# A vision transformer tower on one core: embeddings brought forward, statistics moved to ScalarE, and the first MLP projection from 16-bit halves

## The reference

```
h = concat(class_token, patches @ W.T + b) + pos      # 32 x 37 tokens of 256
x = layernorm(h)
xn = layernorm(x) * ln1_w + ln1_b
q, k = elu(xn @ q_w.T + q_b) + 1, elu(xn @ k_w.T + k_b) + 1 ; v = xn @ v_w.T + v_b   # 16 heads of 16
kv = einsum('bhnd,bhne->bnde', k, v)                  # per token, over the heads
attn = einsum('bhnd,bnde->bhne', q, kv) / einsum('bhnd,bnd->bhn', q, k.sum(heads))
x = x + attn @ o_w.T + o_b
x = x + gelu(( layernorm(x) * ln2_w + ln2_b ) @ fc_w.T + fc_b) @ proj_w.T + proj_b   # MLP, 1024 wide
h = h + x
y = layernorm(h)
scores = softmax(y @ gate_w.T)                        # 16 experts, each takes its top 148 tokens
h = h + experts(y, scores) + shared(y)                # shared: gelu(y @ Sg.T) * (y @ Su.T) @ Sd.T
```

## Time and profile before

| | |
|---|---|
| median of 3 runs | 496.38 us (496.05 to 496.83) |
| the profiled execution | 499.83 us, of which span 498.0 us |
| mean granted clock of TensorE | 0.956 |
| busy, TensorE / its weight loads | 460.0 (92%) / 403.5 (81%) |
| busy, VectorE / ScalarE / GpSimd | 361.9 (73%) / 224.2 (45%) / 150.9 (30%) |
| chain that ended last, by engine | PE 63%, DVE 17%, ACT 5%, issue 5%, DMA 3% |

### The profile page before, as it was taken

The page is one execution under the profiler, slowest core; times in us unless marked ns, Lnnn a source line. Parts: engine busy times, 40 slices in busy tenths (PEclk is TensorE's granted clock), DMA queues, the critical chain, the costliest instruction groups (busy, mean ns, idle before and its releaser), DMA issues.

```text
span 498.0 us, 10363 instructions
## 1 busy us (share of the span) xinstructions
PE 460.0 (92%) x3853; PEld 403.5 (81%) x3853; DVE 361.9 (73%) x674; ACT 224.2 (45%) x527; POOL 150.9 (30%) x252
## 2 busy tenths in 40 slices
PE   7989899999999999899897899899999999999990
PEld 3547678888888888779776679799999999999990
DVE  1289998999999999721398698588876677777720
ACT  1431364664754752324241005555555666565520
POOL 1311032142142221221000052254665444433432
PEclk9988799999999999999699799899999999999995
DMA  7956101101000000000000018977879888898321
GB/s 240 381 219 270 35 1 35 41 4 45 11 6 7 12 11 12 1 11 23 7 2 0 0 30 289 350 283 279 284 282 308 325 326 326 310 323 320 102 28 13
DMA packets 17348, 69.12 MB, mean 139 GB/s; under 512 B 4338, under 2 KB 10399, under 8 KB 12834
## 3 DMA queue, kind: packets, MB, share of 16 engines
q1 hardware_dynamic: 12130, 61.96, 33.3%
q0 software_dynamic: 4608, 5.41, 5.3%
q10 hardware_dynamic: 576, 1.29, 0.7%
HBM read 63.32 MB, written 5.33 MB: 138 GB/s over the span
## 4 chain that ended last, share of the span: by engine, by line
PE 63%; DVE 17%; ACT 5%; issue 5%; DMA 3%; POOL 1%; DVEq 0%; ACTq 0%; POOLq 0%
PE bank L1409 18%; PE bank L1420 13%; PE bank L1182 5%; PE bank L1196 5%; PE bank L1126 4%; DVE qkt L796 4%; PE bank L1211 3%; PE bank L1316 3%; DMA wex_s<-in_wex 3%; DVE scratch L962 3%; DVE scratch L791 2%; PE bank L1141 2%; PE bank L1170 1%; DVE late L810 1%; PE bank L1431 1%
## 5 line engine op out<-in xcount | busy, mean ns | idle before, releaser
L1420 PE MATMUL bank<-scratch,wex_s 128*128 128x148 f32 x512 | 78.6, 297 | 0.2 <-DVE scratch L1054 0.2
L504 POOL DMA_INDIRECT out_rows<-scratch,slot_s x32 | 52.9, 1652 | 85.3 <-DMA out_rows<-scratch,slot_s 64.7
L1420 PEld LDWEIGHTS bank<-scratch,wex_s 128*128 128x128 f32 x512 | 68.4, 192 | 0.5 <-DVE scratch L1054 0.5
L493 POOL DMA_INDIRECT xg<-token_rows,slot_g x32 | 42.1, 1314 | 76.9 <-DVE slot_g L1027 68.1
L725 ACT ACTIVATE scratch<-bank 128x296 f32<-128x296 f32 x64 | 26.6, 416 | 67.7 <-PE bank L1409 67.7
L421 POOL TENSOR_SCALAR tmp<-mv 128x1 f32<-128x1 f32 x30 | 6.7, 223 | 166.0 <-DVE mv L781 166.0
L1409 PE MATMUL bank<-scratch,wsh_s 128*128 128x148 f16 x512 | 53.5, 229 | 0.0
L1409 PE MATMUL bank<-scratch,wfc_s 128*128 128x148 f16 x512 | 52.6, 227 | 0.0
L1409 PE MATMUL bank<-scratch,wproj_s 128*128 128x148 f16 x256 | 50.6, 227 | 0.0
L945 DVE SCALAR_TENSOR_TENSOR wproj_s<-wex_s,wfc_s 128x512 f16<-128x512 f32 x64 | 40.4, 683 | 12.5 <-ACT wfc_s L708 12.5
L1054 DVE SCALAR_TENSOR_TENSOR scratch<-bank,scratch 128x296 f32<-128x296 f32 x64 | 29.4, 460 | 26.4 <-ACT scratch L725 26.0
(11 more groups left out here) (162 smaller groups left out, 907.3 us busy)
## 6 DMA issues: line engine op xcount, KB each, us to landing
wex_s<-in_wex SPq DMA_DIRECT2D x16, 2048.0 KB
wex_s<-in_wex SPq DMA_DIRECT2D x16, 1024.0 KB
patch_s<-in_patches SPq DMA_DIRECT2D x10, 384.0 KB
token_rows<-y_s SPq DMA_DIRECT2D x10, 128.0 KB, 1.7
out_rows<-h_all SPq DMA_DIRECT2D x5, 256.0 KB
wfc_s<-in_wfc SPq DMA_DIRECT2D x1, 1024.0 KB, 5.1
wproj_s<-in_wproj SPq DMA_DIRECT2D x1, 1024.0 KB, 7.1
wsh_s<-in_wsh SPq DMA_DIRECT2D x1, 1024.0 KB, 8.7
```

The source lines that it names most:

```text
L493: gp.indirect_dma_start(xg[b][:], None, rows, bass.IndirectOffsetOnAxis(slot_g[b][:], 0))\
L504: gp.indirect_dma_start(out, bass.IndirectOffsetOnAxis(slot_s[b][:], 0), eo[b], None, compute_op=ALU.add).then_inc(scattered, 16)
L1420: last = pe.matmul(ps_down[k][:, 0:C], wex_s[s.par][:, lo:lo + P], hexT[:, m, :], start=(m == 0), stop=(m == MC - 1))
```

## The change

It does four things.

1. Embeddings come early, through two PSUM banks in turn (`ps_tok(t)` is bank 7 for odd tiles, else bank 0): tiles 2 and 3 ahead of turn 0, 4 to 6 in turn 0, 7 and 8 in turn 1, 9 in turn 2. The keep-busy products behind tile 0's projections go. Router products of tile t-4 go into turn t, and `EARLY` becomes 6.
2. Means and variances move from VectorE to ScalarE: the row sum is the accumulator output of the operation that makes the row (a copy on ScalarE, an addition on VectorE); ScalarE scales it to minus the mean and squares the row with that bias, with a second accumulator output. GpSimd's shift takes one operation less.
3. MLP up works on 16-bit halves: x2 and its weights, scaled by powers of two, are each split into a high and a low half, and three of the four products are summed. The weights are loaded into expert 0's buffer, ScalarE makes the high halves and GpSimd the rests.
4. x2 is transposed in the turn after it is made, ahead of the attention output projection.

```diff
-        EARLY = 7
+        EARLY = 6
-        BESIDE = [6 - r % 2 for r in range(ROUNDS - 1)] + [0]
+        BESIDE = [6] * (ROUNDS - 1) + [0]
...
 @block.sync
             next_patch(Step(0, 2))
+            sp.dma_start(wo_s[:], wo).then_inc(w_in["o"], 16)
+            next_patch(Step(0, 3))
+            sp.dma_start(wfc_raw, wfc.rearrange("p k n -> p (k n)")).then_inc(w_in["fc"], 16)
+            sp.dma_start(wproj_s[:], wproj).then_inc(w_in["proj"], 16)
+            for t in range(4, TILES):
+                next_patch(Step(0, t))
             sp.dma_start(gate_s[:], gate).then_inc(w_in["moe"], 16)
...
+            sp.wait_ge(fclo_made, 2)
             load_gu(Step(0, 0), 0)
...
 @block.gpsimd
+            def rest_of_fc(b):
+                lo, hi = b * nfc // 2, (b + 1) * nfc // 2
+                gp.wait_ge(fchi_made, b + 1)
+                gp.tensor_tensor(wfc16[1][:, lo:hi], wfc_raw[:, lo:hi], wfc16[0][:, lo:hi], ALU.subtract).then_inc(fclo_made, 1)
+            def rest_of_x2(s):
+                gp.wait_ge(x2hi_made, s.times(1, 1))
+                gp.tensor_tensor(x2_16[1][:], x2T[:], x2_16[0][:], ALU.subtract).then_inc(x2lo_made, 1)
...
 @block.scalar
+            def squares(k, t, src, done):
...
+                act.activation(less[:, k, t:t + 1], total[:, k, t:t + 1], ACT.Copy, scale=-1 / D).then_inc(mean_made, 1)
+                act.wait_ge(mean_made, means)
...
+                act.activation(beside[:], src, ACT.Square, bias=less[:, k, t:t + 1],
+                               accum_out=spread[:, k, t:t + 1]).then_inc(done, 1)
             def copy_h(s):
                 act.wait_ge(tok_done, s.times(1, 1))
-                act.activation(h_all[:, s.n, :], ps_tok[:, 0:D], ACT.Copy).then_inc(h_copied, 1)
+                act.activation(h_all[:, s.n, :], ps_tok(s.n)[:, 0:D], ACT.Copy, accum_out=total[:, 0, s.n:s.n + 1]).then_inc(h_copied, 1)
+                act.wait_ge(h_copied, s.times(1, 1))
+                squares(0, s.n, h_all[:, s.n, :], a_stats)
+            def halve_fc():
+                act.wait_ge(w_in["fc"], 16)
+                for b in range(2):
+                    lo, hi = b * nfc // 2, (b + 1) * nfc // 2
+                    act.activation(wfc16[0][:, lo:hi], wfc_raw[:, lo:hi], ACT.Copy, scale=SPLIT)
+                    act.activation(wfc_raw[:, lo:hi], wfc_raw[:, lo:hi], ACT.Copy, scale=SPLIT).then_inc(fchi_made, 1)
             def turn_x2(s):
...
+                act.activation(x2_16[0][:], x2T[:], ACT.Copy).then_inc(x2hi_made, 1)
...
+            def turn(t, soon=(), late_on=(), blocks=()):    # ScalarE's order
+                turn_attn(t-1); norm_a(t+2); scale_xh(t+2); copy_v(t+1); turn_x2(t-2); squares_f(t-3)
+                negate_qk(t+1); exp_qk(t+1); halve_fc() if t == 0; gelu(t-2); copy_h(soon)
+                squares_c(t-1); norm_f(t-3); turn_xn(t+2); turn_y(t-3); copy_h(late_on)
+                gelu_shared(blocks); load_exp() if 2 <= t < TILES - 2; norm_c(t-1)
...
 @block.vector
-            a_moments, c_moments, f_moments
+            def add_attn(s):
+                ve.wait_ge(o_done, s.times(1, 1))
+                ve.wait_ge(x0_made, s.times(1, 1))
+                ve.scalar_tensor_tensor(x_all[:, s.n, :], ps_o[:, 0:D], 1.0, x_all[:, s.n, :], ALU.mult, ALU.add,
+                                        accum_out=total[:, 1, s.n:s.n + 1]).then_inc(x1_made, 1)
+            def add_mlp(s):    # the same from ps_proj and hx into h_all, total[:, 2]
...
 @block.tensor
             def mlp(s):
-                pe.wait_ge(x2T_made, s.times(1, 1))
+                pe.wait_ge(x2hi_made, s.times(1, 1))
+                products = [(k, 0, 0) for k in range(KC)] + [(k, 1, 0) for k in range(KC)] + [(k, 0, 1) for k in range(KC)]
                 for m in range(MC):
-                    for k in range(KC):
-                        last = pe.matmul(ps_fc[m // 4][:, (m % 4) * P:(m % 4 + 1) * P], wfc_s[:, k, m * P:(m + 1) * P],
-                                         x2T[:, k, :], start=(k == 0), stop=(k == KC - 1))
+                    for n, (k, a, b) in enumerate(products):
+                        if m == 0 and n == 2 * KC:
+                            pe.wait_ge(x2lo_made, s.times(1, 1))
+                        last = pe.matmul(ps_fc[m // 4][:, (m % 4) * P:(m % 4 + 1) * P],
+                                         wfc16[a][:, k * MLP + m * P:k * MLP + (m + 1) * P], x2_16[b][:, k, :],
+                                         start=(n == 0), stop=(n == len(products) - 1))
...
             project_qk(Step(0, 0))
-            keep_busy(10)
+            embed(2)
             turn_xh(Step(0, 1))
-            keep_busy(4)
-            embed(Step(0, 2))
+            embed(3)
+            def turn(t, soon=(), late_on=(), blocks=()):
...
+                if t >= 2:
+                    pe.wait_ge(attnT_made, t)
+                    turn_x2(s.off(-2))
...
-                if t >= 1:
-                    turn_x2(s.off(-1))
+                for n in soon:
+                    embed(n)
...
-                if t + 3 < TILES:
-                    embed(s.off(3))
+                if t >= 4:
+                    logits(t - 4)
+                for n in late_on:
+                    embed(n)
                 early(*blocks)
+            turn(0, (4,), (5, 6))
+            turn(1, (7,), (8,))
+            turn(2, (), (9,))
```

More of the change, by code:

```diff
@@ L58 @@
 SPLIT = 256.0
+XSPLIT = 64.0
 HALVES = 8
@@ L124, in vit_tower, with ps_tok @@
         ps_logit, ps_count, ps_prefix, ps_slot = bank[0], bank[1], bank[0], bank[0][:, 320:320 + 4 * E]
+        def ps_tok(t):
+            return bank[7 if t % 2 and t < TILES - 1 else 0]
         def ps_shared(j):
@@ L175, in vit_tower @@
         x2T = sb("x2T", [P, KC, P])
+        x2_16 = [sb(f"x2_16{b}", [P, KC, P], F16) for b in range(2)]
+        col2 = sb("col2", [P, 2 * KC])
         attnT = sb("attnT", [P, KC, P])
@@ L223, in vit_tower @@
         n16 = WGU // HALVES
+        nfc = KC * MLP
+        wfc_raw = wex_s[0][:, 0:nfc]
+        wfc16 = [as16(wfc_s)[:, b * nfc:(b + 1) * nfc] for b in range(2)]
         def w16(par, part, piece):
@@ L372, in _ @@
             load_gu(Step(0, 1), 1)
[L373 to L377, removed]
+            for t in range(TILES):
                 store_y(Step(0, t))
@@ L601, in turn_x2 @@
                 act.wait_ge(x2_turned, s.times(1, 1))
-                affine(x2T, ps_tr, COL_LN2W, COL_LN2B).then_inc(x2T_made, 1)
+                affine(x2T, ps_tr, col2, 0, KC).then_inc(x2T_made, 1)
+                act.wait_ge(x2T_made, s.times(1, 1))
+                act.activation(x2_16[0][:], x2T[:], ACT.Copy).then_inc(x2hi_made, 1)
             def gelu(s):
@@ L678, in _ @@
             norm_f(s9.off(-2))
+            squares_c(s9)
             norm_c(s9)
@@ L875, in turn @@
                 if t >= 1:
-                    c_moments(s.off(-1), after(1))
+                    add_attn(s.off(-1))
                 for j in blocks:
@@ L1115, in add_bias, with embed @@
                 pe.matmul(dst[:, 0:n], ones_b[0:BP, :], bias_s[:, lo:lo + n], start=True, stop=False)
-            def embed(s, part=None):
-                cut = TKC // 2
-                if part != 1:
-                    pe.wait_ge(patch_in[s.par], s.half * 32 + 32)
-                    if not (isinstance(s.n, int) and s.n == 0):
-                        pe.wait_ge(h_copied, s.times(1, 0))
-                    pe.matmul(ps_tok[:, 0:D], sel_s[s.par][:], base_s[:], start=True, stop=False)
-                for k in range(cut if part == 1 else 0, cut if part == 0 else TKC):
-                    last = pe.matmul(ps_tok[:, 0:D], patch_s[s.par][:, k, :], wtok_s[:, k, :], start=False, stop=(k == TKC - 1))
-                if part != 0:
-                    last.then_inc(tok_done, 1)
+            def embed(t):
+                s = Step(0, t)
+                pe.wait_ge(patch_in[s.par], s.half * 32 + 32)
+                if t >= 2:
+                    pe.wait_ge(h_copied, t - 1 if t < TILES - 1 else t)
+                pe.matmul(ps_tok(t)[:, 0:D], sel_s[s.par][:], base_s[:], start=True, stop=False)
+                for k in range(TKC):
+                    last = pe.matmul(ps_tok(t)[:, 0:D], patch_s[s.par][:, k, :], wtok_s[:, k, :], start=False, stop=(k == TKC - 1))
+                last.then_inc(tok_done, 1)
             def turn_xh(s):
@@ L1300, in _ @@
             turn_y(s9.off(-1))
-            early(5, 6)
+            logits(TILES - 3)
+            early(5)
             pe.wait_ge(yT_made, TILES - 1)
-            for t in range(TILES - 1):
-                logits(t)
+            logits(TILES - 2)
             turn_y(s9)
```

205 lines of the change are left out of this document (106 added, 99 removed).

## The result

The changed kernel took 485.44 us (median of 4 runs, 484.01 to 485.78) against 496.61 (median of 4) for the kernel before beside it: ratio 0.9771, 95% interval 0.9749 to 0.9793. It is faster by 11.2, where 19.4 were forecast; the time lies 1.4 above the range. The profiled execution took 485.78 with a span of 484.0.

What follows compares the result with a forecast made beforehand. TensorE bounds turns 0 to 6, VectorE those from 7; after the change VectorE, at 16.2 a turn. Profiled 499.8 - 19.8 + 0.7 = 480.7, less 3.45 for the median 477.3, said 477; own range 472 to 482, with rivals 471 to 484.

Steps and rivals of the forecast that it cites:

- The start: Up to turn 2's value sums: they begin at 57.6 instead of 58.98, upper end 63.6 with the clock lost as before.
- VectorE's turn: One tile-loop turn on VectorE without mean and variance: 16.2 instead of 17.80, range 16.05 to 17.8.
- TensorE's turn: One tile-loop turn on TensorE: 15.9 instead of 18.97, MLP up as 48 16-bit passes taking 2.7 instead of 3.6.
- The first rival, on weight loads: MLP up: 98 ns weight loads bound the 16-bit passes, MLP up 4.7, a turn 16.8, time 486; chance 12%.
- the slower rival: ScalarE's squares need a table of their own, with loads in front of exp and GELU: 500; chance 3%.
- Turns 4 to 7 at 16.0: Middle of the tile loop: VectorE the bound, TensorE still a little behind, 16.0 each, 64.0 together.
- The cover left is the 0.3 by which VectorE is the longer.: Tile-loop turn: ScalarE's statistics before exp end at 7.65, as q and k do; 0.3 of cover, turns settle at 16.2.
- The tail: From turn 9 to the last router product: 47.7 instead of 53.5, ending at 220.5, 19.8 earlier.
- The term of the 16-bit passes: In the last turns: MLP up of three tiles, with no exp in front of GELU, saves 0.9 each, -2.6.
- The clock at the end: Behind the router products: the clock loss stays as before, 0, lower end -2.9.
- Selection and experts: Selection, with one shared block moved behind the router: one more VectorE product and longer TensorE rounds, +0.7, between 0.3 and 1.7.
- the three that ended at 481, 486 and 487: Rivals: dear ScalarE accumulators, 481 (10%); weight loads bounding 16-bit passes, 486 (12%); VectorE's additions eating their saving, 487 (6%).

Runs made afterwards that it cites:

- fp32_up: The changed kernel with the first MLP projection in float32 again, without halves of the weights or of x2: 484.49 us, ratio 0.978.
- pool_order: The changed kernel with norm_a for tile t+3 moved to the head of GpSimd's turn: 478.19 us, ratio 0.9653.
- probe_small: The kernel before with twelve more 128x1 operations, read by nobody, at the end of each GpSimd turn: 495.75 us against 496.08.
- tail_order: pool_order with shared block 4 behind tile 9's x2 transposes and tile 9's yT copy ahead of the exp table load: 473.16 us, ratio 0.9542.
- norm_a_last: pool_order with norm_a for tile t+3 at the end of GpSimd's turn, behind norm_c: 482.61 us, ratio 0.9759.

## Why the prediction was wrong, and where it was right

- *The start* (57.6): right, 56.48. The clock is full there; the halving of the weights and the queue of SP cost nothing (without them, in `fp32_up`, it is 56.80). Turns 2 and 3 (18.5 and 15.3) were 19.24 and 15.57; 0.5 of turn 2's excess are the halves.
- *VectorE's turn* (16.2): right; with nothing in its way it is 15.96. Its accumulator reads are 0.08 and 0.09.
- *TensorE's turn* (16-bit passes of 56 ns): right, 2.68 us to the next operation for 48, and about 1 us of waiting for GELU behind it. The first rival, on weight loads, is out. The 81 ns that the Trainium skill ("TensorE: Matmul & The Clock Gate", Back-to-back issue gap) gives for such pairs is not what happens here: 48 in a row take 56 each.
- *ScalarE's accumulator read* (taken 0.1, 0 to 0.4): 0.19. Squares load no table (16 loads in either kernel); the slower rival is out.
- **Turns 4 to 7 at 16.0: the step that failed.** The working stopped at "The cover left is the 0.3 by which VectorE is the longer." It priced the low half on GpSimd by one row, 0.73, and treated everything else on GpSimd as it was. But the change moves norm_a from the head of GpSimd's turn to just in front of norm_c, and the two together from beside VectorE's reductions to beside its products. Of their ten operations (twelve in the kernel before, 0.19 to 0.57 each) four took 1.8 to 2.7. It cost 7.6 us over the four turns; `pool_order` gives them back, and `probe_small` shows the long operations without the change.
- *Turn 8* (17.4): right, 17.56. The norm_c that its copy of attnT stands behind is the first with no norm_a in front of it.
- *The tail* (47.7): 48.9. The term of the 16-bit passes, -2.6, was too large against the 1.1 set for copy and low half: instead of 1.5 both together brought 0.5, and at tile 9 0.0. The waits named by the trace, 1.34 for yT of tile 9 behind a table load among them, were not in the sum.
- *The clock at the end* (left as it was, lower end -2.9): in the profiled execution it stayed. `tail_order` and `norm_a_last` show that the 2.6 were to be had.
- *Selection and experts* (+0.7): against the profiled execution of the kernel before 3.1 less. From the router's end it was 257.8 there and is 254.7. The stage window 270.00 to 285.00 of the kernel before has a clock of 0.77, the matching one of the changed kernel none of it:

```profile
270.00:285.00 15.00, 11.86 (x55) 9.42 (x56) 9.93 (x33) 0.07 (x1) 0.00 (x0) 0.77 0.00 0
```

```profile
259.00:274.00 15.00, 11.35 (x77) 9.24 (x76) 11.62 (x35) 0.30 (x1) 0.00 (x0) 1.00 0.01 1
```

  One shared block more stands there for TensorE between the rounds, but that is not needed to keep the clock: `probe_small`, with TensorE's program of the kernel before, has 1.00 in that window and takes 253.9 from the router's end. The changed kernel takes 0.8 more than that, near the forecast's 0.7, but its first twelve products also take 5.47 where `probe_small` has 4.58, so one execution of each neither confirms nor refutes a term of this size. The profiled execution of the kernel before was its slowest on record (499.83, clock 0.956; its later runs lie from 492.27 to 498.17, at 0.962 to 0.982). Why one execution loses clock there and another does not stays open.

By terms, on the profiled executions: start -1.1, turns 2 and 3 +1.0, turns 4 to 7 +7.6, turn 8 +0.2, tail +1.2, the rest -3.7: 5.1 above the 480.7. The last term was no luck for the number that was forecast, the median: the sum began with that slow execution and took 3.45 off for it at the end, which is the same loss. The median lies 8.4 above 477, and the first five terms are 8.8. One end of the range was off as well: with its two terms, -2.9 and -0.9, the lower end comes to 473.5 and not to 472.

Of the rivals, the three that ended at 481, 486 and 487 had the right place (turns that stay long) and the wrong cause. That they came nearer than the forecast, 486 nearest of all, is luck. What was not tried: embeddings spread over the turns again, since the new places of their banks and of the router's products hang on the early order. The best kernel here is `tail_order`, 473.16, 4.6% faster than the kernel before.

## What to carry to other kernels

Price the small operations of GpSimd by what VectorE does beside them, not by their mean: look for minimum and maximum of the same form, and for the operation of VectorE that ends when the long one does. When a change moves such a chain, write down for each engine's queue what stands in front of the operation that somebody waits for, also where nothing in the queue was edited but its inputs. And a saving on an engine that waits for the next input anyway (here 16-bit passes) is worth only as much as other work covers the preparation that it asks for.

## What the runs showed of the hardware

- A GpSimd operation of 128 elements, 0.19 us by itself, took up to 2.32 us beside a VectorE product with two SBUF inputs of 2.29, and 0.19 beside reductions of 2.28 with one input.
- It goes the other way too: beside GpSimd's subtraction over 1,024 columns a VectorE product of 2.28 took 4.23. The product with rden, 0.42 in `pool_order`, took 0.70 in the changed kernel, where it began at 120.34 beside GpSimd's hx (0.73 from 120.03).
- The same program of TensorE with the same waits ran at either clock. Behind 1.13, 0.35, 0.88 and 1.34 us of waiting for inputs in the last turns TensorE's twelve products took twice their time in the changed kernel and in `pool_order` (5.47, 1.2 GHz), and their usual 2.84 in `norm_a_last` (2.4 GHz). What decides it, no run here shows.
